# Norm pass and weighting of routed rows on ScalarE, sixteen places for loaded rows

## The reference, cut to what matters

```
x = x + attn(layernorm(x))          # causal, one head of width 1024, 4 x 1024 tokens
z = layernorm(x)
scores = softmax(z @ gate_w.T)      # 8 experts
top_scores, sel = top_k(scores, 2)
# for each of the 8192 (token, choice) pairs, sorted by expert e:
h = silu(z @ w1[e]) * (z @ w3[e])   # 128 -> 256
y = (h @ w2[e]) * score             # 256 -> 128, weighted by the softmax score
x = x + sum of the two y of a token
```

## Time and profile before

| what | value |
|---|---|
| median of three runs | 285.78 us |
| span of the profiled execution | 326.4 us |
| PE, PEld busy | 252.2, 205.5 us |
| DVE busy | 206.5 us |
| ACT busy | 126.1 us |
| POOL busy | 191.3 us |

### The profile page before, as it was taken

One profiled execution on the slowest core, in us unless ns is written; L12 is line 12 of the kernel. 1 busy time (PEld: TensorE's weight loads), 2 busy tenths in 40 slices (PEclk: granted clock), 3 DMA queues, 4 the chain that ended last, 5 costly groups with the idle time before them and its releaser, 6 DMA issues.

```text
span 326.4 us, 5986 instructions
## 1 busy us (share of the span) xinstructions
PE 252.2 (77%) x1618; PEld 205.5 (63%) x1619; DVE 206.5 (63%) x889; ACT 126.1 (39%) x347; POOL 191.3 (59%) x257
## 2 busy tenths in 40 slices
PE   1889999999898999886864376998989898988000
PEld 1767888788667777765742265876767676776000
DVE  1448888676987577863831355675757666666175
ACT  1136665564565546622620112443434343333000
POOL 2437756887888887766377473554545554646100
PEclk9999999999999999999795585999999999999555
DMA  7952112110010111142122121443222222221499
GB/s 228 320 161 65 38 62 77 50 41 27 20 33 33 50 44 35 35 99 71 41 74 66 41 76 49 104 110 84 70 77 69 70 82 65 80 62 43 149 351 294
DMA packets 31111, 28.92 MB, mean 89 GB/s; under 512 B 4328, under 2 KB 25840, under 8 KB 31088
## 3 DMA queue, kind: packets, MB, share of 16 engines
q1 hardware_dynamic: 22512, 17.49, 19.2%
q0 software_dynamic: 4352, 9.05, 8.2%
q10 hardware_dynamic: 4224, 2.10, 2.1%
HBM read 16.40 MB, written 12.22 MB: 88 GB/s over the span
## 4 chain that ended last, share of the span: by engine, by line
PE 56%; POOL 9%; issue 8%; another core or an unknown queue 7%; DVE 7%; DMA 6%; ACT 4%; SPq 1%; POOLq 0%; DVEq 0%
PE scores L490 7%; PE weighed L543 7%; PE weighed L605 5%; PE scores L582 5%; PE scores L584 5%; PE turned L591 5%; POOL expert_rows L396 4%; PE mixed L605 4%; PE scores L583 4%; PE turned L517 4%; DMA XX<-choice_rows 3%; PE scores L574 2%; PE mixed L504 2%; DMA X<-L_attn_in_features 2%
## 5 line engine op out<-in xcount | busy, mean ns | idle before, releaser
L405 POOL DMA_INDIRECT choice_rows<-ysb,ydest x72 | 68.9, 957 | 61.1 <-DVE ysb L942 42.0
L396 POOL DMA_INDIRECT expert_rows<-rows,slots x64 | 65.4, 1022 | 20.1 <-issue 16.1
L714 ACT ACTIVATE sil<-scores 128x256 f32<-128x256 f32 x72 | 27.6, 383 | 83.5 <-PE scores L584 56.3
L582 PE MATMUL scores<-W,xTh 128*128 x72 | 36.6, 508 | 11.4 <-issue 6.1
L922 DVE CAST xTh<-scores 128x128 fp32r<-128x128 f32 x72 | 20.8, 289 | 34.6 <-PE scores L574 19.9
L591 PE MATMUL turned<-identf,g 128*128 128x128 f32 x144 | 29.4, 287 | 13.0 <-DVE g L932 12.7
L543 PE MATMUL weighed<-TL,PT 128*128 128x128 f32 x288 | 38.0, 277 | 1.8 <-DVE X L789 1.8
L490 PE MATMUL scores<-XX,TL 128*128 128x512 f32 (+3 forms) x96 | 36.8, 492 | 1.0 <-ACT TL L694 1.0
L543 PEld LDWEIGHTS weighed<-TL,PT 128*128 128x128 f32 x288 | 34.7, 192 | 2.1 <-issue 2.1
L719 ACT ACTIVATE gTs<-turned 128x256 f32<-128x256 f32 x72 | 27.6, 383 | 21.1 <-PE turned L591 16.2
L591 PEld LDWEIGHTS turned<-identf,g 128*128 128x128 f32 x144 | 18.1, 145 | 22.9 <-DVE g L932 16.4
(11 more groups left out here) (132 smaller groups left out, 528.6 us busy)
## 6 DMA issues: line engine op xcount, KB each, us to landing
xt<-expert_rows SPq DMA_DIRECT2D x72, 66.0 KB
XX<-choice_rows SPq DMA_DIRECT2D x16, 256.0 KB, 5.0
ysb<-L_ffn_w SPq DMA_DIRECT2D x16, 128.0 KB, 2.2
out<-X ACTq DMA_DIRECT2D x8, 256.0 KB, 5.7
choice_rows<-ysb,ydest POOLq DMA_INDIRECT x72
X<-L_attn_in_features SPq DMA_DIRECT2D x2, 512.0 KB, 9.4
expert_rows<-rows,slots POOLq DMA_INDIRECT x64
expert_rows<-padrows SPq DMA_DIRECT2D x1, 528.0 KB
```

Of the source, the lines that this page charges most:

```text
L396: nc.gpsimd.indirect_dma_start(xs, bass.IndirectOffsetOnAxis(ap=slots[:, u, k:k + 1], axis=0), rows[:, u % ROWS_RING, k, :], None).then_in ...
L405: nc.gpsimd.indirect_dma_start(yb, bass.IndirectOffsetOnAxis(ap=ydest[:, q:q + 1], axis=0), ysb[:, q, :], None).then_inc(y_out[q], 16)
L582: mm(bank[2 + j % 2], xTh[:, j % 2, :], hi, start=True, stop=False)
L714: copy(sil[:, j % 2, :], bank[2 + j % 2][:, 0:H], ACT.Silu).then_inc(sil_rdy, 1)
```

## The change

The first norm's pass moves from VectorE to ScalarE. As ScalarE computes scale*x + bias, VectorE now makes a small tensor `shift1` = -mean*rstd for four tiles at once (`shifts1`), one slot after the last statistics of the four, and ScalarE's `norm1` stands at the end of its slot, five slots ahead in place of four. In the expert stage `weighted` moves to ScalarE, behind silu(t) and out_g(t-1). `xt` gets 16 places; a store takes its row numbers from `xt` itself, `ydest` and its copy are gone. So a place of `xt` is free only when the store of its tile has landed, and load t waits for the store of tile t-16 (`y_out`). TensorE's `down(t)` now waits for the weighting of tile t-2. Loops run over 16 tiles; SyncE's are written out.

```
-STAT1_LEAD, NORM1_LEAD, STAT1_GROUP = 9, 4, 4
+STAT1_LEAD, NORM1_LEAD, STAT1_GROUP = 9, 5, 4
-        xt = sb("xt", [P, LANES, ROW])
+        xt = sb("xt", [P, OUT_LANES, ROW])
 # SyncE, load
-                    if not isinstance(m, int) or m >= 1:
-                        sp.wait_ge(y_rdy, m * LANES + j - LANES + 1)
-                    sp.dma_start(xt[:, j, :], xs[ds(r, P), :]).then_inc(xt_in[j], 16)
+                    t = m * LANES + j
+                    q = t % OUT_LANES
+                    if t >= OUT_LANES:
+                        sp.wait_ge(y_out[q], 16 * (t // OUT_LANES))
+                    sp.dma_start(xt[:, q, :], xs[ds(r, P), :]).then_inc(xt_in[q], 16)
...
 # GpSimd, store
-                    yb, bass.IndirectOffsetOnAxis(ap=ydest[:, q:q + 1], axis=0),
+                    yb, bass.IndirectOffsetOnAxis(ap=xt[:, q, COL_DEST:COL_DEST + 1].bitcast(u32), axis=0),
 # TensorE, down
+                else:
+                    pe.wait_ge(y_rdy, t - 1)
 # ScalarE
+            def norm1(u):
+                act.wait_ge(shift1_rdy, u // STAT1_GROUP + 1)
+                wait(act, xx_mm, n_xx(u - 4 - XT_LEAD) if u >= 4 else 0)
+                copy(xn[:, u % 4, :], X[:, token_tile(u), :], ACT.Identity, bias=shift1[:, u:u + 1],
+                     scale=rstd1[:, u:u + 1]).then_inc(xn_rdy, 1)
+            def weighted(r, q):
+                if not isinstance(r, int) or r >= 1:
+                    act.wait_ge(y_out[q], 16 * r)
+                act.wait_ge(y_mm, r * OUT_LANES + q + 1)
+                copy(ysb[:, q, :], product_bank(r, q)[:, 0:D], ACT.Copy,
+                     scale=xt[:, q, COL_W:COL_W + 1]).then_inc(y_rdy, 1)
...
 # VectorE
-            def norm1(u):
-                dve.wait_ge(rstd1_rdy, u // STAT1_GROUP + 1)
-                wait(dve, xx_mm, n_xx(u - 4 - XT_LEAD) if u >= 4 else 0)
-                v.tensor_scalar(xn[:, u % 4, :], X[:, token_tile(u), :], mv1[:, u, 0:1], rstd1[:, u:u + 1],
-                                ALU.subtract, ALU.mult).then_inc(xn_rdy, 1)
+            def shifts1(u0):
+                t = slice(u0, u0 + STAT1_GROUP)
+                dve.wait_ge(rstd1_rdy, u0 // STAT1_GROUP + 1)
+                v.scalar_tensor_tensor(out=shift1[:, t], in0=mv1[:, t, 0], scalar=-1.0, in1=rstd1[:, t],
+                                       op0=ALU.mult, op1=ALU.mult).then_inc(shift1_rdy, 1)
...
+                if is_tile(u1 - STAT1_GROUP) and u1 % STAT1_GROUP == 0:
+                    shifts1(u1 - STAT1_GROUP)
```

More of the change, by code:

```diff
@@ L302, in _ @@
             sp.wait_ge(list_rdy, 1)
-            load(0)
-            with sp.Fori(1, M0 - 1) as m:
+            for m in range(M0 - 1):
                 load(m)
@@ L315, in _ @@
             sp.wait_ge(list_rdy, 2)
-            with sp.Fori(M0, M_TILES) as m:
+            for m in range(M0, M_TILES):
                 load(m)
@@ L608, in down, with weights_of, step, of @@
                 i.then_inc(y_mm, 1)
-            def weights_of(m):
+            def weights_of(t0):
                 _, w = nc.values_load_multi_w_load_instructions(
-                    wcol[0:1, ds(m * LANES, LIST0 + LANES)], engines=[pe.engine], min_val=0,
+                    wcol[0:1, ds(t0, LIST0 + LANES)], engines=[pe.engine], min_val=0,
                     max_val=(E - 1) * WIDE, skip_runtime_bounds_check_because=IN_RANGE)
                 return w
[L617 to L622, removed]
-                    transposes(N_TILES + j)
+            def step(r, q, w):
+                def of(q):
+                    return r + q // OUT_LANES, q % OUT_LANES
+                static, t, j = isinstance(r, int), r * OUT_LANES + q, q % LANES
+                ending = static and t < LANES
+                up(r, q, w[LIST0 + j])
+                if ending and has_xx(N_TILES + t):
+                    transposes(N_TILES + t)
                 if not static or t + 2 < NT:
-                    turn_x(m + (j + 2) // LANES, (j + 2) % LANES)
+                    turn_x(*of(q + 2))
                 if not static or t >= 1:
-                    turn_g(m + (j - 1) // LANES, (j - 1) % LANES)
+                    turn_g(*of(q - 1))
                 if not static or t >= 2:
-                    down(m + (j - 2) // LANES, (j - 2) % LANES, w[LIST0 + j - 2])
-                if m_is_0 and has_tl(N_TILES + j):
-                    projections(N_TILES + j)
-                if m_is_0 and group_at(N_TILES + j, RANK_LAG) is not None:
-                    ranks(group_at(N_TILES + j, RANK_LAG))
+                    down(*of(q - 2), w[LIST0 + j - 2])
+                if ending and has_tl(N_TILES + t):
+                    projections(N_TILES + t)
+                if ending and group_at(N_TILES + t, RANK_LAG) is not None:
+                    ranks(group_at(N_TILES + t, RANK_LAG))
+            def steps(r, q0):
+                w = weights_of(r * OUT_LANES + q0)
+                for q in range(q0, q0 + LANES):
+                    step(r, q, w)
+                return w
             for s in range(1 - XT_LEAD, N_TILES):
@@ L654, in _ @@
             turn_x(0, 1)
[L655 to L656 removed]
+            for q in range(LANES):
+                step(0, q, w)
             pe.wait_ge(place_rdy, NG)
[L658 to L676 removed]
+            steps(0, LANES)
+            for r in range(1, NT0 // OUT_LANES):
+                steps(r, 0)
+                steps(r, LANES)
+            pe.wait_ge(list_rdy, 2)
+            with pe.Fori(NT0 // OUT_LANES, NT // OUT_LANES) as r:
+                steps(r, 0)
+                steps(r, LANES)
+            w = steps(NT // OUT_LANES, 0)
+            turn_g(NT // OUT_LANES, LANES - 1)
+            for q in range(LANES - 2, LANES):
+                down(NT // OUT_LANES, q, w[LIST0 + q])
         @block.scalar
@@ L952, in tile_step @@
                 gated(*of(q))
-                if q >= 2:
-                    weighted(r, q - 2)
                 if more:
@@ L1027, in _ @@
                 tile_step(last, q)
-            for t in range(NT - 2, NT):
-                weighted(t // OUT_LANES, t % OUT_LANES)
             for c in range(NF):
```

121 lines of the change are left out of this document (55 added, 66 removed).

## The result

The changed kernel takes 289.46 us (median of four runs, 289.19 to 289.65) beside 285.27 us of the kernel before (four runs, 284.59 to 285.9): 1.0158 times before, 95% interval 1.0135 to 1.018. On another chip it was 288.98 to 284.52 us, 1.0136 (1.0098 to 1.0174). The forecast was 290.9, +5.1; the ratio makes it +4.5, the medians +4.2.

The account below looks back on a forecast made before the run. The prediction took TensorE to bound attention and GpSimd's indirect DMAs to end the expert stage. Start -0.8, slot 23 +1.1 and gate +4.8 sum to +5.1 on 285.8, giving 290.9 us, range 283.0 to 293.0.

Parts of the forecast that it names:

- The backlog of GpSimd: Expert stage: GpSimd issues one indirect DMA per 1.265 us and is far behind TensorE, store 12 just out at up(28).
- The gate: Expert stage: load t waits for store t-16 to land, so TensorE waits around tiles 25 to 32; +4.8 us, bounds 0 and +5.7.
- the second chain: Tile 32: load 32 waits for the padding write behind load 31, which waits for store 15; delay 6.9 us.
- TensorE's lead: End of the expert stage before the change: last store at 266.2 by TensorE, 267.4 by GpSimd, so GpSimd ends it.
- The start: First norm pass on ScalarE avoids the wait beside GpSimd's memset, first transpose sooner; -0.8 us, bounds -0.84 and 0.
- Slot 23: Attention: VectorE's shift waits for GpSimd's rstd, making norm2, place_rows and a scatter late; +1.1 us, bounds 0 and +1.5.
- ScalarE, cost 0: Expert stage: ScalarE takes the weighting at 0.3 us, 1.07 us per tile, under TensorE's 1.48; no cost.
- Relief counts: Rival, expert loops: VectorE without weighting shortens TensorE's waits; 283.0 us, 22% together with fewer locks.
- Fewer locks: Rival, attention: GpSimd's scatters get shorter without VectorE's norm passes; 283.4 us, counted within the 22% for faster.
- ScalarE the bound: Rival, expert stage: ScalarE's weighting and waits make each tile 0.04 us late; 288.5 us, 8%.
- No gate: Rival, expert stage: stores are never 12 tiles behind, so loads don't wait, and no gain; 286.1 us, 20%.

Follow-up runs that it names:

- ring24: Changed kernel with 24 places for loaded rows instead of 16, load t waiting for store t-24, expert loops written out: 283.97 us, 0.9982 times before.
- copy_kept: Changed kernel with VectorE's copy of the row numbers brought back, so loads don't wait for the store's landing: 283.39 us, 0.9968 times before.
- gate_only: Kernel before plus only the wait of load t for the landing of store t-16; xt keeps 8 places: 290.79 us, 1.0222 times before.
- norm_only: Kernel before with only the first norm's pass on ScalarE and the shifts on VectorE: 283.93 us, 0.9974 times before.
- first_norm_only: Kernel before with only tile 0's norm pass on ScalarE, on a chip where before takes 325.93 us: 325.38 us, ratio 1.000.

## Why the prediction was right, step by step

**The backlog of GpSimd, inferred from a profile that did not show it: right.** The pace of 1.265 us per indirect DMA, taken from the earlier trace rows, holds in every profile (252.64, 253.90, 255.17 in before). GpSimd sets the end before: the lines at the end show it, and so does ring24, where TensorE is 3.5 us faster over the stage than in before (111.7 against 115.2) and the last store does not move (121.5 against 121.6).

**The gate: the right wait at the right tiles, each size a little off.** TensorE's delay at the transpose of tile 28 was forecast as 5.5 us. It is at 188.76 in after and 181.67 in copy_kept, 7.1 later, or 7.3 when both are counted from the first `up` of tile 9, as the prediction counts. For these 1.7 us more, three parts are seen. The transpose came 4.97 us after its store in place of 4.5, 0.5 more (188.76 - 183.79): here the store's landing no longer bound, but the matmuls of tile 26 at half the clock. TensorE was 0.9 us earlier at tile 26, since without the weighting on VectorE the steps behind a new list are shorter (1.75 and 1.99 us at tiles 24 and 32 of copy_kept, where the model had 2.3). And store 12 came 0.4 us later behind tile 9 than forecast: the last group's rows were not ready 0.45 sooner against the first tile (16.6 us behind its `up` in after, 16.5 before). The 0.2 for a wake-up in the 4.5 us came from no row; from a store's landing (173.68 + 2.22) to the load (176.05) it is 0.15.

At tile 32 the forecast had 6.9; 122.0 - 113.8 at the stage's end is 8.1 unrounded, and nothing is given back in between, as forecast. This delay is set by the second chain, through the padding write: the transpose comes 8.4 us after store 15 (187.57 to 195.99) where the forecast had 7.95 (196.15 to 204.1); store 15 landed only at 190.86, 3.3 us behind its issue where 2.22 was taken.

**What TensorE's lead hides.** The prediction had the two engines 1.2 us apart at the end. Measured from the last weighting's end plus the 0.3 of an issue it is 258.95 - 256.85 = 2.1 in before, and 258.52 - 255.13 = 3.4 in copy_kept. Of 8.1 us of delay 3.4 are hidden and 0.6 come back as queueing of the last store, which makes 5.3: the table's 126.8 - 121.5, and the 5.4 of the runs. gate_only adds up in the same way: 7.6 of delay, 2.1 hidden, 0.6 back, 6.1, the table's 127.7 - 121.6. The term was +4.8, within its bounds of 0 and 5.7. It was lowered from 5.7 for pauses that these runs don't have. What made the lowered figure fit is something else: a delay 1.2 us larger than forecast, against a lead 2.2 us larger. That the term came within 0.6 us is in part luck.

**The sum.** The forecast was -0.8 + 1.1 for the norm pass and +4.8 for the gate. Measured are -0.7 for the norm pass (norm_only), -0.2 for the rest of the move, which is within the noise (copy_kept against norm_only), and +5.4 for the gate, +4.5 together. The first two terms were 1.0 us too high and the gate 0.6 too low, so their errors cancel in part; the mechanism that makes the loss is the forecast one.

**The start, -0.8: its sign may hold, its reason fell.** In the second profile of before the norm pass took as long beside the memset:

```profile
9.09 1.83 DVE L773 TENSOR_SCALAR xn<-X,mv,rstd 128x128 f32<-128x128 f32 x1
```

ScalarE's pass in after was done at 7.5 us (6.98 + 0.49), ahead of the memset. But TensorE's first transpose did not wait for `xn` in before (11.13, no idle time, against 0.84 in the earlier trace rows), since the matmuls ahead of it waited for a weight's DMA until 7.56, and until 7.87 in after. The bound of 0 ("a later DMA may bind") is what happened to that row. The Trainium skill (SBUF — State Buffer, Who interferes with whom) has VectorE and GpSimd exclude each other on their shared ports, and the trace agrees for this one pass: 1.83 us, against 0.31 for the next one (of the 32 passes most take 0.33, and three more 0.80 to 1.42). What norm_only gained, 0.7 us, is near the term, and comes from somewhere in attention (the table's first column has 0.4 to 0.6 us, but it varies by as much between kernels of equal attention).

**Slot 23, +1.1: the wait is there, the price is not.** This step failed. VectorE in slot 23 of after, and two steps behind it:

```profile
95.43 0.16 DVE L814 SCALAR_TENSOR_TENSOR shift<-mv,rstd 128x4 f32<-128x4 f32 x1 [3.36 <-POOL rstd L355]
...
96.99 0.65 DVE L847 TENSOR_SCALAR rows<-X,mv,rstd 128x256 f32<-128x256 f32 x1
...
97.85 0.96 POOL L401 DMA_INDIRECT expert_rows<-rows,slots  x1 [0.30 <-issue]
...
98.25 0.17 DVE L909 TENSOR_TENSOR rows<-elog,einv 128x8 f32<-128x8 f32 x1
```

The 3.4 us came as forecast ("about 3 us"). Norm2 (L847) stood at 96.99 where before had 96.45, so it was 0.54 us late, not 1.1. The last step of `place_rows` was late by the same 0.54 (98.25 to 97.71). But no scatter waited for it. GpSimd was still at the rows of the group before, as its budget of scatters per slot has it (97.85 is the fifth of eight of them), and came to the new rows here, 6.2 us after they were done (98.42), and sooner than in before (104.92):

```profile
104.64 1.22 POOL expert_rows L401
```

The scatter in the earlier trace rows, without a gap behind the last step of `place_rows`, I had read as one that waits for it. The row says "0.30 <-issue": the engine was the limit there, not its producer. Counting the scatters, eight to a group, would have shown it.

**ScalarE, cost 0: right, with a wrong price.** The pass took 0.494 us and the weighting 0.368, not 0.3. ScalarE's tile is then 2 x 0.383 + 0.37 = 1.14 us, under 1.48.

**The rivals.** "Relief counts": TensorE did run 1.4 us faster with the weighting gone, but GpSimd's queue swallowed it. Where the gate has used up the lead it can reach the end: the last store comes at 126.8 in after and 127.7 in gate_only. "Fewer locks": a scatter took 1.011 us on average after and 1.016 before, 0.3 us over 64 of them. What VectorE gets back itself was not measured apart and may be part of norm_only's 0.7 us, which is less than half of this rival's 0.8 + 1.6. "ScalarE the bound" falls with copy_kept (its own sum, 285.8 + 72 x 0.04, gives 288.7 and not 288.5). "No gate" falls with gate_only.

## What to carry to other kernels

When a copy that frees a buffer early is taken out, the buffer is held until the slowest consumer's landing; count how far that consumer lags behind at its worst (here 16 tiles), not on average, and make the ring that much deeper or keep the copy. A queue with a fixed pace hides every gain of the engines in front of it, but hands a delay on as soon as its lead is used up. Look for its idle time ahead of its busy stretch (2.4 us here) and move work into that.

## What was not expected of the hardware

**Chips differ.** On one chip the kernel before took 325.93 us (median of 23 runs, 322.29 to 327.72), on the three others of the experiments 284.5. The first profile, with 326.4, looks like that chip's and not like one disturbed execution, which is what the prediction took it for; which chip it came from is not on record. A profile from it (first_norm_only's) has the same long stops, between tiles 11 and 13 above all, in which GpSimd alone goes on (start:end length, busy us of PE, PEld, DVE, ACT, POOL, clock, DMA):

```profile
166.00:182.00 16.00, 5.12 (x16) 3.16 (x16) 2.68 (x12) 1.16 (x3) 10.81 (x12) 0.57 0.19 59
```

What stops four engines there was not settled, nor what the change does there.

**A stall costs clock too.** In after, TensorE's granted clock fell to 0.50, the 1.2 GHz level, behind its waits, and was back at 1.00 by 190 us:

```profile
180.00:182.00 2.00, 0.72 (x4) 0.25 (x3) 0.00 (x0) 0.38 (x1) 1.70 (x2) 1.00 0.51 135
182.00:184.00 2.00, 2.00 (x9) 1.86 (x10) 0.82 (x3) 0.75 (x2) 1.39 (x3) 0.58 0.14 41
184.00:186.00 2.00, 0.76 (x3) 0.08 (x2) 0.00 (x0) 0.38 (x1) 1.70 (x2) 0.50 0.54 134
```

The first `up` matmul takes 0.77 us there instead of 0.48. Most of it hides, since the next load is late anyway. It shows in the 4.97 us from store 12 to the transpose of tile 28, 0.4 more than at tile 25. By tile 32 nothing of it is left to see, as TensorE waits 0.78 us for the load there with the clock at 1.00.

**ScalarE's operations of one size differ in price.** On 128x128 elements a plain copy took 0.28 us, one with a tensor as scale 0.37, one with tensors as scale and bias 0.49. The last also reads X where the others read a matmul's result, and no run tells the two apart.
